# The last adapter job's second product taken in f16 over 98 stacked rows

## What is computed

```python
x = x + _L0_cond_ref(x, fside_Bx8_0, condB_sharedgateprob[:, None], ...)
...
h = relu(x @ w1 + b1)          # 128 -> 32, by language
adapted = h @ w2 + b2          # 32 -> 128
y = x + adapted
out = (y - mean) * rsqrt(var + LN_EPS) * gamma + beta
return x + out
```

## Time and profile before

| what | value |
| --- | --- |
| median of 3 runs | 297.66 us (297.55 to 297.80) |
| the profiled execution's own time | 297.04 us |
| its span, first to last instruction | 295.2 us |
| PE, DVE, ACT, POOL busy in the span | 98%, 91%, 78%, 7% |
| granted TensorE clock, mean | 0.999 of full speed |
| chain that ended last | PE 94%, DVE 2% |

### The profile page before, as it was taken

One profiled execution on the slowest core, in us unless ns is written; L12 is line 12 of the kernel. 1 busy time (PEld: TensorE's weight loads), 2 busy tenths in 40 slices (PEclk: granted clock), 3 DMA queues, 4 the chain that ended last, 5 costly groups with the idle time before them and its releaser, 6 DMA issues.

```text
span 295.2 us, 5086 instructions
## 1 busy us (share of the span) xinstructions
PE 290.1 (98%) x1510; PEld 144.3 (49%) x1510; DVE 268.8 (91%) x585; ACT 231.1 (78%) x517; POOL 19.3 (7%) x32
## 2 busy tenths in 40 slices
PE   8999999999999999999999999999999999999995
PEld 2444444444444444444444444444444444588883
DVE  5999999998989898988989999999999999977795
ACT  6998878788878787877897788887878876667771
POOL 3200201100000000000002010001100011000011
PEclk9999999999999999999999999999999999999999
DMA  6973110244000000000011001010001110000001
GB/s 208 385 307 109 52 65 19 62 120 112 2 2 0 0 2 0 0 2 1 1 22 26 18 9 39 12 25 19 17 3 39 27 18 10 2 36 3 0 2 36
DMA packets 17940, 13.39 MB, mean 45 GB/s; under 512 B 11486, under 2 KB 15994, under 8 KB 17914
## 3 DMA queue, kind: packets, MB, share of 16 engines
q1 hardware_dynamic: 17482, 12.86, 14.4%
q10 hardware_dynamic: 432, 0.21, 0.2%
HBM read 11.23 MB, written 1.05 MB: 42 GB/s over the span
## 4 chain that ended last, share of the span: by engine, by line
PE 94%; DVE 2%; DMA 1%; SPq 1%; issue 1%; ACT 0%; POOL 0%; POOLq 0%; DVEq 0%
PE moe_ps L449 10%; PE moe_ps L446 10%; PE moe_ps L447 10%; PE gate_ps L400 10%; PE up_ps L426 10%; PE up_ps L431 10%; PE up_ps L423 10%; PE gate_ps L403 10%; PE gate_ps L408 10%; DMA w_full<-weights 1%; DVE hidden L680 1%; PE adapt_ps L458 0%; DVE gx_lo L649 0%; SPq L319 0%; DVE h_lo L686 0%
## 5 line engine op out<-in xcount | busy, mean ns | idle before, releaser
L563 ACT ACTIVATE silu<-gate_ps 128x512 f32<-128x512 f32 (+1 forms) x160 | 88.2, 551 | 45.3 <-PE gate_ps L408 44.3
L680 DVE SCALAR_TENSOR_TENSOR hidden<-silu,up_ps 128x512 f32<-128x512 f32 (+1 forms) x160 | 100.3, 627 | 19.2 <-PE up_ps L431 11.6
L686 DVE TENSOR_TENSOR h_lo<-hidden,h_hi 128x512 f16<-128x512 f32 (+1 forms) x160 | 102.4, 640 | 0.2
L568 ACT ACTIVATE h_hi<-hidden 128x512 f16<-128x512 f32 (+1 forms) x160 | 92.8, 580 | 9.2 <-DVE hidden L680 8.4
L426 PE MATMUL up_ps<-gx_lo,w_hi 128*128 128x512 f16 (+1 forms) x160 | 57.3, 358 | 0.4 <-DVE gx_lo L649 0.4
L400 PE MATMUL gate_ps<-x_hi,w_hi 128*128 128x512 f16 (+1 forms) x160 | 57.4, 359 | 0.0
L431 PE MATMUL up_ps<-gx_hi,w_lo 128*128 128x512 f16 (+1 forms) x160 | 57.3, 358 | 0.0
L423 PE MATMUL up_ps<-gx_hi,w_hi 128*128 128x512 f16 (+1 forms) x160 | 57.3, 358 | 0.0
L403 PE MATMUL gate_ps<-x_lo,w_hi 128*128 128x512 f16 (+1 forms) x160 | 57.3, 358 | 0.0
L446 PE MATMUL moe_ps<-h_hi,w_hi 128*128 128x512 f16 (+1 forms) x160 | 57.3, 358 | 0.0
L449 PE MATMUL moe_ps<-h_lo,w_hi 128*128 128x512 f16 (+1 forms) x160 | 57.3, 358 | 0.0
(11 more groups left out here) (88 smaller groups left out, 148.6 us busy)
## 6 DMA issues: line engine op xcount, KB each, us to landing
w_full<-weights SPq DMA_DIRECT2D x8, 768.0 KB, 9.2
affine_sb<-affine SPq DMA_DIRECT2D x16, 128.0 KB, 2.9
x_full<-xT SPq DMA_DIRECT2D x3, 256.0 KB, 8.6
x<-x_blocks SPq DMA_DIRECT2D x48, 16.0 KB, 1.8
out_dram<-result SPq DMA_DIRECT2D x3, 256.0 KB, 2.1
w_full<-weights SPq DMA_DIRECT2D x4, 128.0 KB, 3.0
w_full<-w2b SPq DMA_DIRECT2D x24, 16.0 KB
w_full<-weights SPq DMA_DIRECT2D x1, 256.0 KB, 3.8
```

Source lines behind the costliest of these rows:

```text
L563: nc.scalar.activation(silu_slot(n), gate_ps[n % 2][:, 0:STEPS[n][4]], ACT.Silu, scale=1.0 / W_SCALE).then_inc(silu_ready, 1)
L568: nc.scalar.activation(h_slot(h_hi, n), hidden_slot(n), ACT.Copy).then_inc(h_hi_ready, 1)
L680: nc.vector.scalar_tensor_tensor(out=hidden_slot(n), in0=silu_slot(n), scalar=HIDDEN_RESCALE, in1=up_ps[n % 2][:, 0:STEPS[n][4]], op0=ALU. ...
L686: nc.vector.tensor_tensor(h_slot(h_lo, n), hidden_slot(n), h_slot(h_hi, n), ALU.subtract).then_inc(h_lo_ready, 1)
```

## The change

The half job takes the path of the other three. Its two batches' w2 is loaded as 98 rows (four DMAs for each batch where there was one), ACT's relu writes h_full, `h_upper` is added at ACT's step 151, ahead of `copy_x2`, and `h_others` at DVE's step 151. `w2_upper` and `w2_lower` run at steps 139 and 141, so ahead of the job. The products move from PE's step 153 to 154, and with them `norm_stats` and what follows it, one step later. One add of 256 columns takes the place of two of 128. The widths of the four preparing operations are now 256 columns in this job.

```diff
 def back_at(j):
-    return 6
+    return 6 if j < MOVED else 7
+def w2_at(j):
+    return 0 if j < MOVED else -8
...
-                    if t == last_tile:
+                    if t == last_tile and q >= TAIL[1]:
                         sp.dma_start(stacked(w2b2_sb, q, D, A + 1), w2b2_q).then_inc(adapter_loaded, 16)
...
             def adapter_back(j):
                 _, first, count, _ = JOBS[j]
                 pe.wait_ge(ones_ready, 3)
-                if j < MOVED:
-                    pe.wait_ge(w2_lower_ready, j + 1)
-                    pe.wait_ge(h_others_ready, 2 * (j + 1))
...
-                pe.wait_ge(adapt_h_ready, count)
-                pe.wait_ge(x2_ready, 1)
+                pe.wait_ge(w2_lower_ready, j + 1)
+                pe.wait_ge(h_others_ready, 2 * (j + 1))
+                if j >= MOVED:
+                    pe.wait_ge(x2_ready, 1)
                 for q in range(first, first + count):
-                    last = nc.tensor.matmul(cols(back_ps[q % 2], q // 2, D), stacked(adapt_h, q, S, A + 1),
-                                            stacked(w2b2_sb, q, D, A + 1), start=True, stop=True)
+                    last = nc.tensor.matmul(cols(x2_ps, q, D), cols(h_stack, q, S, STACK), cols(w2_stack, q, D, STACK),
+                                            start=True, stop=True)
...
-                    if n == at and j < MOVED:
+                    if n == at + w2_at(j):
                         w2_upper(j)
                     if n == at + in_at(j) + 1:
                         adapter_relu(j)
-                    if n == at + in_at(j) + 2 and j < MOVED:
+                    if n == at + in_at(j) + 2:
                         h_upper(j)
...
-                if since == 2 and j < MOVED:
+                if since == w2_at(j) + 2:
                     w2_lower(j)
-                if since == 4 and j < MOVED:
+                if since == (in_at(j) + 3 if j < MOVED else in_at(j) + 2):
                     h_others(j)
...
-                if j >= MOVED:
-                    nc.vector.tensor_tensor(cols(y, q, D), cols(back_ps[q % 2], q // 2, D), cols(x2, q, D),
-                                            ALU.add).then_inc(y_ready, 1)
```

More of the change, by code:

```diff
@@ L200, in build @@
         x2_ps = bank("x2_ps")
-        back_ps = [adapt_ps, x2_ps]
         last_tile = TILES - 1
@@ L276, in adapter_count @@
         def adapter_count(t):
-            return 16 * BATCHES * (6 * (t + 1) if t < last_tile else 6 * t + 3)
+            return 16 * (6 * BATCHES * (t + 1) if t < last_tile else 6 * (B - TAIL[2]) + 3 * TAIL[2])
         def fourth(tensor, q):
@@ L519, in _ @@
                 if i == 0:
-                    pe.wait_ge(adapt_h_ready, JOBS[-1][2] + 1)
+                    pe.wait_ge(adapt_h_ready, 1)
                 else:
@@ L574, in adapter_relu @@
                 for q in range(first, first + count):
[L575 to L580, removed]
+                    nc.scalar.activation(cols(h_full, q, S, A), fourth(adapt_ps, q)[:, 0:S], ACT.Relu,
+                                         bias=fourth(b1_sb, q)[:, 0:1]).then_inc(h_full_ready, 1)
             def w2_upper(j):
@@ L585, in w2_upper @@
                     act.wait_ge(back_done, j)
-                nc.scalar.activation(w2_stack[:, :], w2_full[:, :], ACT.Copy, scale=W_SCALE).then_inc(w2_upper_ready, 1)
+                width = JOBS[j][2] * D
+                nc.scalar.activation(w2_stack[:, 0:width], w2_full[:, 0:width], ACT.Copy,
+                                     scale=W_SCALE).then_inc(w2_upper_ready, 1)
             def h_upper(j):
                 act.wait_ge(h_full_ready, BEFORE[j + 1])
-                nc.scalar.activation(h_stack[0:A, :], h_full[:, :], ACT.Copy, scale=H_SCALE).then_inc(h_upper_ready, 1)
+                width = JOBS[j][2] * S
+                nc.scalar.activation(h_stack[0:A, 0:width], h_full[:, 0:width], ACT.Copy,
+                                     scale=H_SCALE).then_inc(h_upper_ready, 1)
             def copy_x2(j):
@@ L705, in w2_lower @@
                 dve.wait_ge(w2_upper_ready, j + 1)
-                nc.vector.scalar_tensor_tensor(out=w2_stack[2 * A:STACK - 1, :], in0=w2_full[2 * A:STACK - 1, :], scalar=W_SCALE,
-                                               in1=w2_stack[2 * A:STACK - 1, :], op0=ALU.mult,
+                width = JOBS[j][2] * D
+                nc.vector.scalar_tensor_tensor(out=w2_stack[2 * A:STACK - 1, 0:width], in0=w2_full[2 * A:STACK - 1, 0:width],
+                                               scalar=W_SCALE, in1=w2_stack[2 * A:STACK - 1, 0:width], op0=ALU.mult,
                                                op1=ALU.subtract).then_inc(w2_lower_ready, 1)
@@ L711, in h_others @@
                 dve.wait_ge(h_upper_ready, j + 1)
-                nc.vector.tensor_scalar(h_stack[2 * A:3 * A, :], h_full[:, :], H_SCALE, None, ALU.mult).then_inc(h_others_ready, 1)
-                nc.vector.scalar_tensor_tensor(out=h_stack[A:2 * A, :], in0=h_full[:, :], scalar=H_SCALE, in1=h_stack[0:A, :],
-                                               op0=ALU.mult, op1=ALU.subtract).then_inc(h_others_ready, 1)
+                width = JOBS[j][2] * S
+                nc.vector.tensor_scalar(h_stack[2 * A:3 * A, 0:width], h_full[:, 0:width], H_SCALE, None,
+                                        ALU.mult).then_inc(h_others_ready, 1)
+                nc.vector.scalar_tensor_tensor(out=h_stack[A:2 * A, 0:width], in0=h_full[:, 0:width], scalar=H_SCALE,
+                                               in1=h_stack[0:A, 0:width], op0=ALU.mult,
+                                               op1=ALU.subtract).then_inc(h_others_ready, 1)
             def norm_stats(j, i):
@@ L723, in norm_stats @@
                         dve.wait_ge(x2_ready, 1)
-                    if j < MOVED:
-                        nc.vector.scalar_tensor_tensor(out=y[:, :], in0=x2_ps[:, :], scalar=OUT_RESCALE, in1=x2[:, :],
-                                                       op0=ALU.mult, op1=ALU.add).then_inc(y_ready, BATCHES)
-                if j >= MOVED:
-                    nc.vector.tensor_tensor(cols(y, q, D), cols(back_ps[q % 2], q // 2, D), cols(x2, q, D),
-                                            ALU.add).then_inc(y_ready, 1)
+                    width = JOBS[j][2] * D
+                    nc.vector.scalar_tensor_tensor(out=y[:, 0:width], in0=x2_ps[:, 0:width], scalar=OUT_RESCALE,
+                                                   in1=x2[:, 0:width], op0=ALU.mult,
+                                                   op1=ALU.add).then_inc(y_ready, JOBS[j][2])
                 if i == 0:
```

## The result

The changed kernel is slower, and the forecast of +0.67 us lies inside the measured interval. Its median is 298.17 us (22 runs, 297.65 to 299.26) against 297.77 us (22 runs, 296.74 to 298.56) of the kernel before, measured beside it. The ratio is 1.002 with an interval of 1.0011 to 1.0029, which on 297.77 is 0.60 us, and 0.33 to 0.86. (The two medians alone are 0.40 apart.) How near the size came to the forecast is therefore read from the traces, one execution of each kernel.

What follows compares the result with a forecast made beforehand. PE's matmuls were taken to bound the kernel (94% of the chain). Products -0.52 + 0.11 and waiting +1.08 gave +0.67 us; on the runs' scale 297.66 + 0.67 = 298.33, say 298.3, range 297.5 to 298.7.

Steps and rivals of the forecast that it cites:

- Products: On PE, two f32 products leave step 153 (-0.52 us) and two f16 ones cost 0.11 at step 154; alone -0.41.
- Weights: Extra DMAs on SP, w2_upper and w2_lower on ACT and DVE: cost nothing, a delay of some 0.2 gone within two steps.
- ACT: Step 151: h_upper takes 0.42, next operation starts 0.30 later; silu(152) ends at 280.84, gate(154) starts at about 280.90.
- DVE: Step 151: h's first part takes 0.29 us and its second 0.42, running after h_lo(150) ends at 280.46.
- The collision: POOL's x2_beta, from 280.64, holds the shared port; h's second part on DVE stands still until 281.24, ending 281.65.
- the rival in which VectorE wins the pair: h's second part takes the port before x2_beta; gate(155) at 282.48, +0.24 us, time 297.90; chance 22%.
- hidden(152), up(154), gate(155): On DVE and PE after the standstill: starts at 281.68, 282.15 and 282.91, the last +0.67 us against 282.24.
- Who wins the pair: Deciding point on the shared port: POOL's x2_beta leads h's second part by 0.17 and wins, nearer the winning row.
- The end: Norm work a step later on DVE leaves the last h_lo some 0.1 us to spare: cost nothing, otherwise 0.2.
- The 0.1 that the forecast added for this case: If h's first part ran in a two-port mode, x2_beta would wait for its end at 280.78: some 0.1 more.

Runs made afterwards that it cites:

- Experiment 5: Changed kernel with h_upper at ACT's step 153, h_others at DVE's 154, products at PE's 156, scaling and results behind the loop: 297.48 us, ratio 0.9989.
- experiment 3: Kernel before, with the half job's f16 weights also loaded and made but not used: 297.81 us, ratio 0.9994.
- experiment 1: Changed kernel with POOL's x2_beta of the half job held until both other parts of h are made: 297.65 us, ratio 1.0003.
- experiment 4: Kernel before with its two f32 products at PE's step 154 instead of 153 and the norm work a step later: 297.90 us, ratio 1.0003.
- 6: Changed kernel with the copy of x2 ahead of h_upper and x2_beta held until both other parts of h are made: 298.16 us, ratio 1.0015.
- experiment 10: Changed kernel with h_others at DVE's step 152 and PE's wait for h_others put behind that for x2: 298.07 us, ratio 1.0012.
- experiment 2: Changed kernel with ACT's copy of x2 ahead of h_upper at step 151: 298.54 us, ratio 1.0026.
- experiment 7: Changed kernel with h_others at DVE's step 152, behind hidden(152) and h_lo(151): 298.35 us, ratio 1.0025.
- experiment 9: Experiment 5 with PE's wait for h_others put behind that for x2, last ahead of the products: 297.27 us, ratio 0.9989.

## Why the prediction was right

The mechanism and the size came as forecast, +0.70 against +0.67 by the traces; by the runs' times the size is known less sharply, 0.33 to 0.86. Point by point:

- *Products.* -0.52 + 0.11 was said. Experiment 5 shows the -0.52 at gate(155), the changed kernel 0.12 for the two new ones.
- *Weights.* They were to cost nothing. One hidden was to come some 0.2 late and the delay to be gone in a step or two. In experiment 3 hidden(142) is 0.31 late and hidden(147) not at all, and nothing is left at the end.
- *ACT.* h_upper 0.42, and 0.30 until the next starts: measured 0.40 and 0.31. With the traces' offset of 0.41, the forecast 279.90 for its start is 280.31, where it stands. gate(154), forecast at 280.90, stands at 281.30, 0.01 early.
- *DVE.* The first part was put at 0.29 and the second at 0.42, both from job 0's wider forms by halving: 0.28 and, undisturbed in experiment 1, 0.42.
- *The collision.* x2_beta forecast for 280.64, so 281.05 with the offset, and there it stands. DVE was to stand still until 0.60 after that; it was 0.58. The second part's 0.84 is the "about 0.8" of the forecast. Experiment 1 shows that taking the collision away takes 0.43 away, to +0.27; the text had +0.24 for that case, as the rival in which VectorE wins the pair.
- *hidden(152), up(154), gate(155).* 281.68, 282.15, 282.91 plus 0.41 are 282.09, 282.56, 283.32; measured 282.09, 282.57, 283.35. The last 0.03 are the products' 0.12, and pieces of 0.01 of PE's pace.
- *Who wins the pair* was the point at which it could have turned, and the lead was forecast as 0.17; it was 0.16, and POOL won. The rows had a lost pair at 0.04 and a won one at 0.26, and 0.17 was given to the nearer of the two; here the forecast had no more than that, and so its rival had 22%.
- *The end.* 0.1 to spare was said. The last h_lo ended at 288.97 + 0.99 = 289.96 and the last matmul, in its place at pace, started at 290.12. So it sufficed; experiment 4 shows how thin it is, since without PE's delay the same move costs 0.12, and in experiments 1, 6 and 10, with PE late by 0.27 to 0.43, some 0.04 was lost there. (The forecast put the last matmul of the kernel before at 288.97; its trace has it at 289.01.)

One sentence of it was left open and turned out to matter. The forecast held the first part, which reads one tensor, to be free of the port unless it ran in a two-port mode, and named no row for the case. Experiments 2 and 6 showed that it stands still like the second. The 0.1 that the forecast added for this case did not come: the first part ended at 281.18, x2_beta is recorded from 281.05, and yet its 0.72 did not grow, and DVE went on 0.58 after its start, where it was 0.59 in experiment 2. Why x2_beta did not wait for the first part there stays open. But the finding closes the obvious repair, an earlier x2_beta, which only moves the standstill from the second part to the first.

So the answer to where 0.41 us of saved matmul time went: hidden(152) came later by more than PE had gained. The experiments take the loss apart at up(154), which waits for it, by its starts shown above. A shift is against the 6.66 of the kernel before:

| what stands ahead of hidden(152) | up(154) less hidden(147) | shift |
| --- | --- | --- |
| nothing new, the f32 products gone (experiment 5) | 281.76 - 275.63 = 6.13 | -0.53 |
| h_upper on ACT (experiment 7) | 281.30 - 274.88 = 6.42 | -0.24 |
| and the two parts on DVE, x2_beta out of their way (experiment 1) | 281.52 - 274.72 = 6.80 | +0.14 |
| and x2_beta beside them (the change) | 282.57 - 275.34 = 7.23 | +0.57 |

So h_upper costs 0.29, the two operations on DVE 0.38 and the collision 0.43, together 1.10; with the new products' 0.12 behind up(154) gate(155) is at +0.70, within 0.01. Less than half of this is the port. The rest is work that stands ahead of hidden(152) however the pair falls.

## What to carry to other kernels

When work leaves the bounding engine but needs preparation elsewhere, look at which values the bounding engine takes next from those engines and how long ahead they are made: here the change lost 0.7 us with the preparation in a step where PE waited for hidden already, and gained 0.24 to 0.28 with it two and three steps later. When an operation of ScalarE is put ahead of one that releases GpSimd, check which VectorE operations GpSimd's will then fall on, and prefer one that reads PSUM or one whose result is not needed soon. And put the wait that is released last at the end of a list of waits: it was worth 0.12 us ahead of the matmul in experiment 10, though nothing at the end of the program in experiment 9.

## What was not expected of the hardware

- A tensor_scalar of one f32 input in SBUF to f16 (32x256) stands still beside a GpSimd tensor_tensor: 0.62 instead of 0.28 us.
- The standstill ends before GpSimd's operation is recorded to end: 0.57 to 0.59 after its start, of 0.72 or 0.73, in the changed kernel and in experiments 1 and 2. GpSimd won with a recorded lead of 0.16, 0.23 and 0.25; with 0.04 it had lost. What decides between 0.04 and 0.16 no run shows.
- Exchanging two waits ahead of a matmul, so that the one released last is also the last in order, moved its start from 0.26 to 0.14 us (and to at most 0.15 in experiment 9) behind the release.
- The first 275 us of the program, in kernels that differ there in the half job's weights at most, took between 274.72 and 276.65 us over the twelve traces. Comparing spans of two single executions would have put 0.5 us too much on the change; a common instruction as the zero took that out.
